# A graph layer on one Trainium2 core: the second group's transposes behind the first selection, the read-back on the other queue, ranks read by two engines, and a one-hot one use later

## The chip, the cores and the metric

One core of one Trainium2 chip runs the whole kernel. The metric is the device time of one execution in microseconds (us), the median of several runs.

## The reference

For 8 graphs of N = 1024 nodes with C = 128 features, and an adjacency matrix of 0 and 1:

```python
h = jnp.maximum(_layernorm(x, axis=-1), 0.0)
# per node: the first S = 25 neighbours by index
scores = jnp.where(A != 0, -jnp.arange(N), neg_inf)
vals, idx = jax.lax.top_k(scores, S)
feats = jnp.where((vals > neg_inf)[..., None], h[idx], neg_inf)
agg = feats.max(axis=2)
agg = jnp.where((degree <= S)[..., None], jnp.maximum(agg, 0.0), agg)
out = jax.nn.relu(jnp.concatenate([h, agg], axis=-1) @ W + b)
x + out
```

## The kernel before

The 8192 nodes are worked on in 16 groups of 512 rows, two groups to a graph (a batch). A group's way is this. The 0/1 adjacency is made a bf16 `mask`, and turned so that the neighbour index lies on the partitions (`mask_t`, 8 blocks of 128). **Selection**: `place(g, k)` on TensorE writes running counts of block k into the PSUM bank `side`, and `choose(g, k)` on ScalarE turns them into `chosen`, 1 where a neighbour is among the first 25. Block k + 1 needs `chosen` of block k, so this is a chain of TensorE and ScalarE. **Read-back**: `chosen` is stored to the DRAM tensor `kept` block by block and read back as `picks`, in which the neighbours of a partition are of another class (index modulo 8 instead of block). **Ranks**: `ranks` multiplies `picks` by `half_w` into one of two PSUM banks `ring`, and ScalarE (`stage`) reads it into `rank`, the running number of a neighbour in its class partition. **Picks**: for rank t = 1 to 4 and four pairs of classes, VectorE makes one-hots (`make_hot`, all 8 classes at once), `pick_pair` multiplies h (a high and a low f16 part) with them into `picked`, two buffers in turn, and `take_pair` on VectorE takes the maximum into `best`. The 16 pairs are called uses 0 to 15; the first two are copied by ScalarE (`first_maxima`). **Late ones**: neighbours of rank above 4 are marked in `late`, skewed over the partitions by seven DMAs of SP (`skew_late` into `late_skew`), ranked again (`late_ranks`), and picked in a loop whose length is read from data (`late_round` on TensorE; `take_late` and `make_late_hot` on VectorE). The first late one-hots are made ahead of that loop behind the uses in `LATE_HOT_USES`. At the end `project` multiplies by W, and `finish_group` adds x.

The order on each engine is written out by hand, and engines wait for each other by counting semaphores only. In the loop over groups, `step` interleaves: in uses 4 to 15 of group g lie ranks of group g + 1 (uses 6 to 13) and the selection of group g + 2 (uses 7 to 14). POOL makes h of the next batch in the odd groups but the last (`normalize`: lines 385, 388 and 391, then `fold_count`, then `low_part`, line 373, which writes `h_lo`); VectorE makes the high part behind use 10.

Ahead of the loop stands a prologue, in which groups 0 and 1 have no earlier work to hide behind. Their masks are turned by TensorE (`turn_blocks(g, q)`, 8 transposes for each quarter q) and copied out of PSUM. What the steps of the prediction touch, in the order of each engine:

- TensorE (lines 692 to 713): the transposes of group 0; `place(0, k)`, with `turn_blocks(1, 0)` to `(1, 2)` behind places 5, 6 and 7 and `(1, 3)` after them; two places of group 1; the 8 ranks of group 0, each of which waits for both halves of the read-back (`first_loaded`, line 602); then pairs 0 to 3 with places 2 to 5 of group 1 among them, places 6 and 7, and four late ranks.
- ScalarE (lines 502 to 524): two copies; `choose(0, k)` and the store of block k on ScalarE's own DMA queue; the square root of the variances (`spreads`) behind block 2; the read-back of the first 64 partitions (`first_picks(0)`, waits for the stores of blocks 0 to 3) behind block 6 and of the others (`first_picks(1)`, waits for blocks 4 to 7) behind block 7; two selections of group 1; the 8 rank reads; the rest of group 1's selection.
- VectorE (lines 864 to 908): the masks of group 0, two copies, statistics of x, the gain, W and the bias in parts, the masks of group 1 (line 781), h's high and low part, four copies for group 1 (line 897), the masks of group 2, then `make_hot(1, 0)`, which waits for all 8 rank reads, `make_hot(2, 0)`, and the late classes (lines 903 and 905).
- SP (lines 304 to 327): the loads; from line 315 it waits for the read-back, loads x of batch 1, turns the masks of group 2 by DMA, skews the late classes, stores group 1's `second_chosen` (it lies in `late_hot`) block by block, and reads it back (line 302).

## Time and profile before

| | us |
|---|---|
| median of 3 runs | 674.34 (673.2 to 675.48) |
| the profiled execution | 675.0 |
| its span, first to last instruction | 673.3 |
| busy in it: TensorE | 595.0 |
| VectorE | 601.3 |
| ScalarE | 403.3 |
| POOL (GpSimd) | 95.1 |

The profile is one execution. Busy times are unions over an engine's instructions; DMA-issuing, semaphore and register instructions are not counted as busy. PE is TensorE's matmul part and PEld its weight load, DVE is VectorE, ACT ScalarE, SP the queue that issues most DMAs. A row of the timeline has the start, the duration, the engine, the line, the operation, the tiles as out<-in, a count when neighbouring instructions are merged, and in brackets how long the engine had stood idle before it and what released it. The mean granted clock of TensorE over the span is 0.982 of full speed.

### The profile page before, as it was taken

What the parts mean: (1) busy time and instruction counts of PE and PEld (TensorE: products, weight loads), DVE (VectorE), ACT (ScalarE), POOL (GpSimd) and SP (SyncE); (2) the same over time, 40 slices, a digit from 0 to 9 for tenths busy, and PEclk for the clock granted to TensorE, in tenths of its full rate; (3) what the DMA queues carried; (4) which work ended last, traced back from release to release, by engine and by line L of the source; (5) the groups of instructions that cost most, each with busy time, mean ns of one, the idle gap of its engine ahead of it and who ended that gap; (6) DMA issues with size and microseconds to landing.
All of it is one profiled execution on the core that took longest, in us unless ns stands there. A gap on an engine that the chain in (4) does not pass through costs nothing.

```text
span 673.3 us, 9821 instructions
## 1 busy us (share of the span) xinstructions
PE 595.0 (88%) x2800; PEld 248.5 (37%) x2800; DVE 601.3 (89%) x727; ACT 403.3 (60%) x556; POOL 95.1 (14%) x142
## 2 busy tenths in 40 slices
PE   4457989899998999899998999899998999899986
PEld 2212334344433434343343434344443434343333
DVE  4844978999999999999999999999999999999996
ACT  3245855768277664857667685858667674836310
POOL 1300003200060000500051001500050000600000
PEclk9959999999999999999999999999999999999998
DMA  8456785658458383576657484566657352240100
GB/s 341 162 129 218 281 237 186 208 108 299 92 204 238 133 254 91 201 212 227 187 195 218 136 273 125 207 181 232 179 200 227 103 184 60 74 163 21 63 16 17
DMA packets 99438, 115.81 MB, mean 172 GB/s; under 512 B 66003, under 2 KB 85718, under 8 KB 94934
## 3 DMA queue, kind: packets, MB, share of 16 engines
q1 hardware_dynamic: 98102, 113.41, 53.1%
q10 hardware_dynamic: 1312, 2.10, 1.1%
q8 instruction: 12, 0.20, 0.1%
q14 instruction: 12, 0.10, 0.0%
HBM read 58.85 MB, written 20.97 MB: 119 GB/s over the span
## 4 chain that ended last, share of the span: by engine, by line
issue 40%; PE 25%; DVE 19%; POOL 8%; DMA 3%; ACT 3%; DVEq 1%; SPq 0%; POOLq 0%; ACTq 0%
DVE best L826 9%; PE picked L640 8%; PE picked L641 7%; PE ring L567 4%; DVE best L832 4%; POOL h L391 3%; DVE late_hot L838 2%; POOL h L385 2%; POOL h L388 2%; DVE hot L813 2%; PE final L667 1%; DMA picks<-kept 1%; PE final L671 1%; DMA adj_in<-in_adj_dram 1%; ACT late_rank L458 1%
## 5 line engine op out<-in xcount | busy, mean ns | idle before, releaser
L826 DVE TENSOR_TENSOR best<-picked,best 128x1024 f32<-128x1024 f32 x224 | 268.7, 1217 | 21.2 <-PE picked L641 20.2
L640 PE MATMUL picked<-hot,h_hi 128*128 128x512 f16 x512 | 196.3, 383 | 23.9 <-DVE best L826 14.7
L641 PE MATMUL picked<-hot,h_lo 128*128 128x512 f16 x512 | 196.0, 383 | 0.0
L640 PE MATMUL picked<-late_hot,hi_skew 128*128 128x512 f16 x344 | 130.5, 379 | 13.8 <-DVE late_hot L838 9.8
L641 PE MATMUL picked<-late_hot,lo_skew 128*128 128x512 f16 x344 | 130.3, 379 | 0.0
L458 ACT ACTIVATE rank<-ring,late_bias 128x512 bf16<-128x512 f32 x128 | 87.6, 688 | 52.6 <-PE ring L567 52.4
L832 DVE TENSOR_TENSOR best<-picked,best 128x1024 f32<-128x1024 f32 x86 | 105.1, 1222 | 15.4 <-PE picked L641 14.9
L458 ACT ACTIVATE late_rank<-ring,late_bias 128x512 bf16<-128x512 f32 x128 | 81.4, 687 | 57.4 <-PE ring L567 57.3
L466 ACT ACTIVATE chosen<-side,bias_cut 128x512 bf16<-128x512 f32 x120 | 81.9, 682 | 21.5 <-PE side L596 21.5
L640 PEld LDWEIGHTS picked<-hot,h_hi 128*128 128x128 f16 x512 | 50.3, 98 | 102.4 <-DVE best L826 32.9
L495 ACT COPY best<-picked 128x1024 f32<-128x1024 f32 x32 | 32.4, 1014 | 92.3 <-PE picked L641 92.3
L813 DVE TENSOR_SCALAR hot<-rank 128x4096 f16<-128x4096 bf16 x64 | 77.8, 1217 | 9.5 <-ACT rank L458 9.5
L838 DVE TENSOR_SCALAR late_hot<-late_rank,numbers 128x2048 f16<-128x2048 bf16 x86 | 75.2, 875 | 0.0
L641 PEld LDWEIGHTS picked<-hot,h_lo 128*128 128x128 f16 x512 | 50.4, 99 | 50.5 <-issue 1.6
L477 ACT ACTIVATE late<-rank,bias_late 128x1024 bf16<-128x1024 bf16 x60 | 63.8, 1136 | 0.0
L640 PEld LDWEIGHTS picked<-late_hot,hi_skew 128*128 128x128 f16 x344 | 33.4, 97 | 75.6 <-DVE late_hot L838 23.4
L411 POOL TENSOR_SCALAR late_other<-late_most 1x1 f32<-1x1 f32 x64 | 16.0, 251 | 285.7 <-DVE late_most L818 280.6
L567 PE MATMUL ring<-picks,half_w 128*128 128x512 bf16 x128 | 50.3, 395 | 5.3 <-DMA picks<-kept 4.3
L385 POOL TENSOR_TENSOR h<-x_in,moments 128x1024 f32<-128x1024 f32 x8 | 15.2, 1902 | 262.9 <-DVE gain L809 262.9
L453 ACT ACTIVATE mask<-adj_in 128x1024 bf16<-128x1024 uint32 x52 | 50.6, 1051 | 0.0
L596 PE MATMUL side<-mask_t,select_w 128*128 128x512 bf16 x120 | 47.5, 396 | 0.5 <-ACT mask_t L504 0.5
L595 PE MATMUL side<-mask_t,rest_w 128*128 128x512 bf16 x105 | 42.0, 400 | 5.9 <-ACT chosen L466 4.6
(85 smaller groups left out, 474.1 us busy)
## 6 DMA issues: line engine op xcount, KB each, us to landing
adj_in<-in_adj_dram SPq DMA_DIRECT2D x15, 2048.0 KB, 8.9
picks<-kept SPq DMA_DIRECT2D x15, 1024.0 KB, 5.0
kept<-chosen SPq DMA_DIRECT2D x112, 128.0 KB, 2.8
late_skew<-late SPq DMA_DIRECT2D x32, 192.0 KB, 3.4
x_in<-in_x_dram SPq DMA_DIRECT2D x8, 512.0 KB, 6.3
late_skew<-late SPq DMA_DIRECT2D x16, 256.0 KB, 4.6
late_skew<-late SPq DMA_DIRECT2D x32, 128.0 KB, 3.5
xres<-in_x_dram SPq DMA_DIRECT2D x16, 256.0 KB, 2.7
```

What stands on the lines that cost most here:

```text
L453: nc.scalar.activation(mask[:, q, :], counts, ACT.Sign).then_inc(mask_made, 1)
L458: nc.scalar.activation(dst[:, k, :], ring[k % 2][:, :], ACT.Relu, bias=bias).then_inc(ring_read, 1)
L466: nc.scalar.activation((second_chosen if second else chosen)[:, k, :], side[:, :], ACT.Sign, bias=bias_cut[:, 0:1], scale=-1.0).then_inc(c ...
L477: nc.scalar.activation(late[:, 2 * p:2 * p + 2, :], rank[:, s, 2 * p:2 * p + 2, :], ACT.Sign, bias=bias_late[:, 0:1]).then_inc(late_made, 1)
L567: last = nc.tensor.matmul(ring[k % 2][:, :], w[:, :], m, start=(i == 0), stop=(i == len(terms) - 1))
L596: nc.tensor.matmul(side[:, :], select_w[:, :], turned[:, k, :], start=(k == 0), stop=True, skip_group_check=True).then_inc(place_written, 1)
L640: nc.tensor.matmul(dst, hi[:, slot, k, :], onehot, start=start, stop=False)
L641: return nc.tensor.matmul(dst, lo[:, slot, k, :], onehot, start=False, stop=stop)
L813: nc.vector.tensor_scalar(hot[:, (t - 1) % 3, :, :], rank[:, s, :, :], float(t), None, ALU.is_equal).then_inc(hot_made, 1)
L826: nc.vector.tensor_tensor(best[:, half, s, :, :], picked[s][:, :, :], best[:, half, s, :, :], ALU.max).then_inc(picked_read, 1)
L832: nc.vector.tensor_tensor(best[:, s, i, :, :], picked[i][:, :, :], best[:, s, i, :, :], ALU.max).then_inc(late_read[i], 1)
L838: nc.vector.tensor_scalar(late_hot[:, part, :], late_rank[:, part, :], which, None, ALU.is_equal).then_inc(late_hot_made[i], 1)
```

## The change

The constant `LATE_HOT_USES` goes from (12, 14) to (13, 14): the first half of the late one-hots is made behind `take_pair` of use 13 instead of 12, in every group. The rest changes the prologue alone. TensorE does all transposes of group 1 behind the whole selection of group 0, then three places of group 1 instead of two, and waits for the read-back in front of its ranks. The ranks of group 0 are read by two engines, the even classes by ScalarE, which counts two at a time, and the odd ones by VectorE with an addition and a maximum on a semaphore of its own, `first_ranked`. ScalarE takes the square root behind block 1 instead of 2, and no longer issues the read-back; SP does, in two halves as before, ahead of its wait for `normed_made`, and waits for the landing only ahead of `store_chosen`. VectorE makes the masks of group 1 right behind the gain, ahead of the parts of W and of the bias.

```diff
--- before.py
+++ after.py
@@ -54,7 +54,7 @@
         return [[k for k in range(K) if use == first + k * (last - first + 1) // K] for use in range(USES)]
 
     SELECT_WITH, RANK_WITH = spread_over(7, 14), spread_over(6, 13)
-    LATE_EARLY, LATE_WITH, COUNT_WITH, COUNT_USE, LATE_HOT_USES = 4, {4: (4, 5), 5: (6, 7)}, (6, 7), 8, (12, 14)
+    LATE_EARLY, LATE_WITH, COUNT_WITH, COUNT_USE, LATE_HOT_USES = 4, {4: (4, 5), 5: (6, 7)}, (6, 7), 8, (13, 14)
     LATE_USES, HIGH_USE, TURN_USE = {14: (0, 1), 15: (2, 3)}, 10, 15
     STATS_USES, MOMENTS_USE, GAIN_USE = (9, 10), 12, 5
 
@@ -179,6 +179,7 @@
         first_stored = [sem(f"first_stored{i}") for i in range(2)]
         first_loaded = sem("first_loaded")
         ring_read = sem("ring_read")
+        first_ranked = sem("first_ranked")
         late_clamped = sem("late_clamped")
         late_made = sem("late_made")
         late_skewed = sem("late_skewed")
@@ -292,6 +293,12 @@
                     sp.wait_ge(chosen_made, chosen_due)
                     sp.dma_start(kept_by_block[k], (second_chosen if first else chosen)[:, k, :]).then_inc(chosen_stored, 16)
 
+            def first_picks(i):
+
+                part = slice(i * (P // 2), (i + 1) * (P // 2))
+                sp.wait_ge(first_stored[i], 16 * HALF)
+                sp.dma_start(picks[part, :, :], kept_by_class[part]).then_inc(first_loaded, 16)
+
             def load_picks(ranked):
 
                 sp.reg_add(stored_due, stored_due, LANDED)
@@ -312,13 +319,15 @@
             load_adj(1, 1)
             sp.wait_ge(mask_made, Q)
             load_adj(2, 0)
-            sp.wait_ge(first_loaded, 32)
+            for i in range(2):
+                first_picks(i)
             sp.wait_ge(normed_made, 1)
             load_x(1)
             for q in range(Q):
                 sp.wait_ge(mask_made, 2 * Q + q + 1)
                 sp.dma_start_transpose(mask_t[:, :, q * P:(q + 1) * P], mask[:, q, :]).then_inc(mask_turned, 16)
             skew_late(0)
+            sp.wait_ge(first_loaded, 32)
             store_chosen(True)
             load_picks(K)
             load_xres(0, 0)
@@ -465,12 +474,6 @@
                 act.wait_ge(place_written, g * K + k + 1)
                 nc.scalar.activation((second_chosen if second else chosen)[:, k, :], side[:, :], ACT.Sign, bias=bias_cut[:, 0:1], scale=-1.0).then_inc(chosen_made, 1)
 
-            def first_picks(i):
-
-                part = slice(i * (P // 2), (i + 1) * (P // 2))
-                act.wait_ge(first_stored[i], 16 * HALF)
-                act.dma_start(picks[part, :, :], kept_by_class[part]).then_inc(first_loaded, 16)
-
             def find_late(p, s, ranked):
 
                 act.wait_ge(ring_read, ranked)
@@ -504,21 +507,19 @@
                 nc.scalar.copy(mask_t[:, 2 * n:2 * n + 2, :], turned_bank[n]).then_inc(block_copied[0], 1)
             for k in range(K):
                 choose(0, k)
-                if k == 2:
+                if k == 1:
                     spreads(0)
                 act.wait_ge(chosen_made, k + 1)
                 act.dma_start(kept_by_block[k], chosen[:, k, :]).then_inc(first_stored[k // HALF], 16)
-                if k == K - 2:
-                    first_picks(0)
-            first_picks(1)
-            for k in range(2):
+            for k in range(3):
                 choose(1, k)
-            for k in range(K):
-                stage(0, k, rank[:, 0], late_bias[:, 0:1])
+            for k in range(0, K, 2):
+                act.wait_ge(ring_written, k + 1)
+                nc.scalar.activation(rank[:, 0, k, :], ring[0][:, :], ACT.Relu, bias=late_bias[:, 0:1]).then_inc(ring_read, 2)
             for s in range(2):
                 first_maxima(0, s, 0)
-                choose(1, 2 + s)
-            for k in range(4, K):
+                choose(1, 3 + s)
+            for k in range(5, K):
                 choose(1, k)
             for k in range(LATE_EARLY):
                 stage(K, k, late_rank, late_bias[:, k:k + 1])
@@ -598,9 +599,7 @@
 
             def ranks(g, at, k):
 
-                if isinstance(g, int) and g == 0:
-                    pe.wait_ge(first_loaded, 32)
-                elif k == 0:
+                if k == 0:
                     pe.wait_ge(picks_loaded, 16 * g)
                 accumulate(at, k, [(half_w, picks[:, k, :])])
 
@@ -695,20 +694,22 @@
                 turn_blocks(0, q)
             for k in range(K):
                 place(0, k)
-                if k >= K - 3:
-                    turn_blocks(1, k - (K - 3))
-            turn_blocks(1, Q - 1)
+            for q in range(Q):
+                turn_blocks(1, q)
             pe.wait_ge(chosen_made, K)
-            for k in range(2):
+            for k in range(3):
                 place(1, k)
+            pe.wait_ge(first_loaded, 32)
             for k in range(K):
-                ranks(0, 0, k)
+                if k > 1:
+                    pe.wait_ge(*((first_ranked, k // 2) if k % 2 else (ring_read, k)))
+                nc.tensor.matmul(ring[k % 2][:, :], half_w[:, :], picks[:, k, :], start=True, stop=True).then_inc(ring_written, 1)
             pe.wait_ge(lo_made, 1)
             for use in range(PAIRS):
                 pick_pair(0, use, 0)
-                place(1, 2 + use)
-            for k in range(2 + PAIRS, K):
-                place(1, k)
+                place(1, 3 + use)
+            place(1, K - 1)
+            pe.wait_ge(first_ranked, HALF)
             for k in range(LATE_EARLY):
                 late_ranks(0, K, k)
 
@@ -869,6 +870,8 @@
             stats_of(0, range(K))
             moments_of(0)
             make_gain(0)
+            for q in range(Q):
+                next_mask(1, q)
             dve.wait_ge(weights_loaded, 64)
             nc.vector.tensor_scalar(w_scaled[:, :, :], w_in[:, :, :], 1.0 / SCALE, None, ALU.mult).then_inc(consts_made, 1)
 
@@ -888,8 +891,6 @@
             dve.wait_ge(bias_step, 8)
             for q in range(Q):
                 nc.vector.tensor_copy(bias_parts[:, q * C:(q + 1) * C], bias_sum[:, 2, :]).then_inc(consts_made, 1)
-            for q in range(Q):
-                next_mask(1, q)
             high_part(0, 0)
             first_low()
             for n in range(PAIRS):
@@ -897,6 +898,10 @@
                 nc.vector.tensor_copy(rank[:, 1, 2 * n:2 * n + 2, :], turned_bank[n]).then_inc(second_copied, 1)
             for q in range(Q):
                 next_mask(2, q)
+            for k in range(1, K, 2):
+                dve.wait_ge(ring_written, k + 1)
+                nc.vector.tensor_scalar(rank[:, 0, k, :], ring[1][:, :], late_bias[:, 0:1], 0.0, ALU.add, ALU.max).then_inc(first_ranked, 1)
+            dve.wait_ge(first_ranked, HALF)
             dve.wait_ge(ring_read, K)
             make_hot(1, 0)
             make_hot(2, 0)
```

## Rows read from the trace of the kernel before

**Rows 1.** The page: busy time by engine; costliest groups; durations of one line (min/median/max).

```profile
PE 595.0 (88%) x2800; PEld 248.5 (37%) x2800; DVE 601.3 (89%) x727; ACT 403.3 (60%) x556; POOL 95.1 (14%) x142
...
L826 DVE TENSOR_TENSOR best<-picked,best 128x1024 f32<-128x1024 f32 x224 | 268.7, 1217 | 21.2 <-PE picked L641 20.2
...
L838 DVE TENSOR_SCALAR late_hot<-late_rank,numbers 128x2048 f16<-128x2048 bf16 x86 | 75.2, 875 | 0.0
...
L838 DVE TENSOR_SCALAR late_hot<-late_rank,numbers x86: 737/744/2362, 77.8 to 662.6; 128x2048 f16<-128x2048 bf16 x86
```

**Rows 2.** The chain of waits, its first 50 us: start, duration, what.

```profile
31.23 3.61 DMA kept<-chosen
34.86 4.64 DMA picks<-kept
...
45.86 1.24 DVE hot L813
```

**Rows 3.** The timeline of the prologue, 19 to 32 us.

```profile
19.00 1.90 POOL L385 TENSOR_TENSOR h<-x_in,moments 128x1024 f32<-128x1024 f32 x1 [16.45 <-DVE gain L809]
...
22.05 0.69 ACT L466 ACTIVATE chosen<-side,bias_cut 128x512 bf16<-128x512 f32 x1 [1.13 <-PE side L596]
...
26.04 2.48 DVE L781 TENSOR_SCALAR mask<-adj_in 128x1024 bf16<-128x1024 int32 x4
...
28.70 0.69 ACT L466 ACTIVATE chosen<-side,bias_cut 128x512 bf16<-128x512 f32 x1 [5.96 <-PE side L596]
...
30.27 1.47 PE L577 MATMUL picked<-eye,mask 128*128 128x128 bf16 x16
```

**Rows 4.** The timeline of an odd group, 110 to 125 us, VectorE and POOL.

```profile
110.72 3.58 DVE L826 TENSOR_TENSOR best<-picked,best 128x1024 f32<-128x1024 f32 x3
...
110.87 1.90 POOL L385 TENSOR_TENSOR h<-x_in,moments 128x1024 f32<-128x1024 f32 x1 [36.91 <-DVE gain L809]
...
120.29 2.12 POOL L373 TENSOR_TENSOR h_lo<-h,h_hi 128x1024 f16<-128x1024 f32 x1
...
120.60 2.36 DVE L838 TENSOR_SCALAR late_hot<-late_rank,numbers 128x2048 f16<-128x2048 bf16 x1
...
122.88 2.34 DVE L826 TENSOR_TENSOR best<-picked,best 128x1024 f32<-128x1024 f32 x2
```

**Rows 5.** DMA issues, us to landing: blocks 6, 7 and 3 of the first selection.

```profile
kept<-chosen ACTq DMA_DIRECT2D x1, 128.0 KB, 1.7
...
kept<-chosen ACTq DMA_DIRECT2D x1, 128.0 KB, 3.6
...
kept<-chosen ACTq DMA_DIRECT2D x1, 128.0 KB, 3.2
```

**Rows 6.** The first ranks: timeline; groups; a window (busy, PEclk, DMA share, GB/s).

```profile
39.55 1.03 PE L567 MATMUL ring<-picks,half_w 128*128 128x512 bf16 x2 [2.41 <-DMA picks<-kept]
...
40.20 1.27 ACT L458 ACTIVATE rank<-ring,late_bias 128x512 bf16<-128x512 f32 x2 [2.33 <-PE ring L567]
...
41.65 1.27 ACT L458 ACTIVATE rank<-ring,late_bias 128x512 bf16<-128x512 f32 x2 [0.19 <-PE ring L567]
...
L845 DVE SCALAR_TENSOR_TENSOR xres<-final,xres 128x512 f32<-128x512 f32 x16 | 11.1, 692 | 5.9 <-PE final L671 5.9
...
39.00:46.00 7.00, 4.52 (x8) 0.76 (x8) 0.14 (x1) 5.07 (x8) 0.00 (x0) 0.50 0.86 189
```

**Rows 7.** The timeline of group 0, use 6: the first rank of group 1.

```profile
66.92 0.39 PE L567 MATMUL ring<-picks,half_w 128*128 128x512 bf16 x1 [1.87 <-DMA picks<-kept]
```

**Rows 8.** The late skews of an odd group: timeline, and the last one's us to landing.

```profile
131.51 0.59 SPq L256 DMA_DIRECT2D late_skew<-late  x1
...
late_skew<-late SPq DMA_DIRECT2D x1, 192.0 KB, 3.7
...
135.92 0.59 PE L567 MATMUL ring<-late_skew,half_w 128*128 128x512 bf16 x2
...
137.78 0.10 PEld L567 LDWEIGHTS ring<-late_skew,half_w 128*128 128x128 bf16 x1 [0.68 <-ACT late_rank L458]
```

## The prediction

> **What bounds the kernel now.** I read the busy shares first: VectorE and TensorE are busy 89% and 88% of the span [rows 1], so the steady part is two nearly full engines that hand `picked` tiles to each other, and an idle microsecond inside it is rare. The unfilled time is at the front, so I read the chain of waits for its first 50 us: a store of 3.61 us, its read-back of 4.64 us, and the first VectorE one-hot only at 45.86 [rows 2]. The timeline of that stretch says why the store is late: ScalarE's selection of group 0 ran at a pitch of 0.69 + 1.13 = 1.82 us up to 22.05, then waited 5.96 us [rows 3]. TensorE had been put on `turn_blocks(1, 0)`, which waits for a mask that VectorE makes at 26.04, because the parts of the bias come first. Then I looked in the steady part for instructions much longer than their fellows: `late_hot` has 86, median 744 ns, longest 2362 ns [rows 1]. The mean of 875 ns gives (875 - 744) x 86 / (2362 - 744) = 7 long ones, one in each odd group that makes a new batch's h. There POOL's `h_lo` runs from 120.29 to 122.41, and the late_hot that starts at 120.60 ends at 122.96 [rows 4].
>
> **The front, step by step.** (a) With the transposes of group 1 behind `place(0, 7)`, blocks 6 and 7 follow at the pitch of 1.82: starts at 22.05 + 1.82 = 23.87 and 25.69, end 26.38. Before, block 7 was stored from 31.23 [rows 2]: 4.8 us earlier. The sqrt and its table load only move from behind block 2 to behind block 1, so one selection pays for it either way (nothing).
> (b) The read-back's halves move to SP. Before, the first half was issued on ScalarE's own queue between the stores of blocks 6 and 7; block 6 landed in 1.7 us, block 7 in 3.6 us [rows 5]. Block 3 is issued near 19.1 and lands 3.2 us later [rows 5], so SP can ask for the first half near 22.3, and it is nearly done when block 7 goes out at 26.4. I take 1.7 us, a landing at 28.1; the upper end is 3.6 (30.0). The second half, then 4.64 us as before [rows 2], lands at 32.8, at worst 34.7. Behind SP's wait stand x(1) and the mask transposes; they were behind the same landing before, so nobody loses. x(1) now shares the engines with the half: up to 0.5 us, by the distance between 1.7 and 3.6.
> (c) ScalarE no longer stands in a wait for stores, so `choose(1, 0..2)` run meanwhile. TensorE is free of group 0 at 25.7. The 32 transposes cost 1.47 us for 16 [rows 3] at the faster pace, up to 1.4 times that at the slower: 28.6 to 29.8. One copy (taken as one of the four masks that last 2.48 us together [rows 3]) and three place/choose rounds, two at 1.45 to 1.82, bring the third place to 33.0 to 34.2. It now stands ahead of the ranks in TensorE's order, so ranks start when the later of it and the read-back is there: I take 33.7, against 39.55 [rows 6].
> (d) VectorE makes the four masks from about 17.1, beside POOL's normalisation, which starts some 1.9 us earlier than 19.00 [rows 3], since the sqrt is one block earlier. The late_hot of 2362 ns [rows 4] shows that one of the two engines can wait out the other. Even all in series (2.5 us of masks, 6.9 us of POOL) the masks are there before 25.7 and h is ready by 27; the cover is some 2 us. If it is gone, each us counts in full.
> (e) Ranks split over two engines: less than it looks. A bank's round is read (0.69), signal, matmul: from ScalarE's 40.20 to 41.65 it is 1.45 us [rows 6], with only 0.19 us of idle, and two readers don't shorten a bank's round. What goes is ScalarE's turn on the second bank. VectorE reads 128x512 of PSUM in 692 ns [rows 6]. The last rank is ready 0.65 + 0.4 + 3 x 1.45 + 0.69 = 6.1 us after the start, against 45.86 - 39.55 = 6.3. The granted clock was 0.50 there (the 1.2 GHz level) [rows 6], after TensorE had stood idle for most of its wait for the read-back. Now it comes from transposes and places; at 2.4 GHz a round is some 0.2 us shorter, 5.0 us in all. I take 5.8.
> First one-hot: 33.7 + 5.8 = 39.5, which is **6.4 us earlier**; bounds 33.0 + 5.0 = 38.0 (7.9 us) and 34.9 + 6.2 = 41.1 (4.7 us).
> (f) Who carries it on: behind the one-hots SP issues seven skews and eight stores without a gap, then reads group 1's picks back, and TensorE waits 1.87 us for them at 66.92 [rows 7]. All of this hangs on the one-hots and on SP, so it moves with them. The last place of group 1 leaves the end of that chain (one fewer to do), but SP is later there: nothing more.
>
> **The late one-hots, steady part.** In an odd group with a new batch, take 12 ends at 120.65; `late_hot(0)` sits out POOL's `h_lo`. After the change take 13 goes there. It reads PSUM and one tile of SBUF, and three of its kind while POOL wrote `h` from 110.87 to 112.78 took 3.58 us, against 2.34 for two elsewhere [rows 4]. So take 13 runs 120.7 to 121.9, `late_hot(0)` waits for the same end and finishes at the same 122.96, and one take, a pair's 2.34 less one's mean of 1.21 to 1.22 = **1.13 us**, is gone from the path [rows 1, 4].
> What is late next: `late_skew`, whose making depends on ScalarE and SP, not on take 13, and stays where it is. The last of seven is issued at 131.51 and lands 3.7 us later, at 135.2; TensorE used it at 135.92 [rows 8]. So TensorE can come only some 0.6 us earlier there, not 1.13. But the second pair of these matmuls stood 0.68 us for ScalarE at 137.78, by its weight load [rows 8], and ScalarE's reads move by the full 1.13, so most of the lag is taken up: I take 1.03 us a group. Bounds: 0.5 (the lag goes through) and 1.13. Seven groups: **7.2 us**, from 3.5 to 7.9. In the other nine groups `late_hot(0)` and take 13 only change places while VectorE runs without a gap: nothing, within 0.1 each.
>
> A rule to weigh: the Trainium skill (SBUF — State Buffer, "SBUF: two separate sides") has it that VectorE in a two-port mode or with two SBUF inputs and GpSimd take one port pair for a whole instruction, and the other "fully blocks". The trace agrees for late_hot (2362 ns beside 744). By it a take, with one SBUF input, is free of this; if its SBUF input did count, rival B would hold.
> A rule that speaks against (b): the Trainium skill (DMA: Bandwidth & Descriptors, "Rules for kernel authors") says that spreading transfers over issuing engines doesn't help bandwidth, as they share the 16 engines. By it block 7 would gain only what the earlier start of the first half gives; this case's 1.7 and 3.6 us cannot tell the two apart.
>
> **Sum.** The profiled execution took 675.0 us, its span 673.3; the median of the runs is 674.34. 675.0 - 6.4 - 7.2 = 661.4, which is 660.7 on the median's scale. The known ends are 674.34 - 7.9 - 7.9 = 658.5 and 674.34 - 4.7 - 3.5 = 666.1.
>
> **Rivals.**
> A: the skews hold the steady part, each odd group gives 0.5. For: 135.2 against 135.92. Against: the idle time at 137.78. It gives 674.34 - 6.4 - 3.5 = 664.4.
> B: POOL's `h_lo` stops take 13 too (or late_hot meets the same delay elsewhere), so the one-hots give nothing: 674.34 - 6.4 = 667.9. Against: the takes from 110.72.
> C: the front gives little, since VectorE's early masks and POOL block each other, or the ranks wait for place(1, 2), or the second half lands late. With 3 us of the 6.4: 674.34 - 3 - 7.2 = 664.1; with nothing: 667.1.
> D, slower: TensorE's clock. It was at 0.50 from 39 to 46 [rows 6] (the 1.2 GHz level), after a stretch in which the engine mostly waited. Group 0's first matmuls now lie among places and ranks in another rhythm. If the level stayed low into group 0's uses, each matmul costs 1.03 - 0.61 = 0.42 us of pitch instead of 0.59 - 0.38 = 0.21 [rows 6, 8]; the 13.6 us are used up after 65 more matmuls at the low level. A whole group 0 (48 for its twelve uses and some 40 for its late rounds) would make 674.34 - 13.6 + 18.5 = 679.2. Against: the same dense picks follow behind the one-hots as before, and over the whole span TensorE's clock hardly shows below full.
> E: the change does not do what it says, because the order on TensorE leaves the wait at a mask (masks later than 25.7 + 4.8): 667, as C's end.
>
> **Chances.** Forecast 0.62; A 0.14; B 0.08; C and E 0.12; D 0.04. The range that holds 8 in 10 takes the sum's known ends, and half of B and C: 658.0 to 667.0. Below 0.3% (2 us) this kernel's measurement can't tell a change from none; the cases give faster 0.95, within 0.3% 0.02, slower 0.03.
>
> **What would show it.** ScalarE's blocks 6 and 7 at 23.9 and 25.7 with no wait of 5 us; the store of block 7 under 2.5 us; ranks from 33 to 34.5; the first one-hot at 39.5; TensorE's wait for picks in group 0 as long as before, all 6.4 us earlier. In odd groups a take beside `h_lo` of 1.22 us, then a late_hot of about 1.1 us, and a period of two groups 1.0 us shorter; TensorE waiting for `late_skew` there shows the lag. I am wrong on the front if masks of group 1 come after 25.7 or the second half lands after 35, and on the steady part if the longest take grows past 1.3 us or VectorE stands idle before the takes of the next group by what it saved.

## The result, and the profile after

The changed kernel takes 662.66 us (median of 5 runs, 660.67 to 664.44), the kernel before 674.34 us (672.96 to 675.48) beside it: a ratio of 0.9827, 95% interval 0.9804 to 0.9850. The forecast was 660.7 us in a range of 658.0 to 667.0. The profiled execution of the new kernel took 664.44 us with a span of 661.5, against 675.0 and 673.3.

The page of the kernel after (busy time by engine; then the take and the late one-hot, busy us and mean ns of one):

```profile
PE 596.5 (90%) x2800; PEld 249.8 (38%) x2800; DVE 597.0 (90%) x731; ACT 401.7 (61%) x552; POOL 96.3 (15%) x142
...
L827 DVE TENSOR_TENSOR best<-picked,best 128x1024 f32<-128x1024 f32 x224 | 270.0, 1218 | 23.3 <-PE picked L640 21.9
...
L839 DVE TENSOR_SCALAR late_hot<-late_rank,numbers 128x2048 f16<-128x2048 bf16 x86 | 66.5, 773 | 0.0
```

Against [rows 1], TensorE's busy time is 1.5 us longer, and VectorE's is 4.3 us shorter: the late one-hots lost 8.7 us (75.2 to 66.5), but four rank reads and the lengthened masks came in. Two parts can be told apart by where each group's result is added on VectorE (the read of `final` into `xres`, start in us):

| group | 0 | 1 | 3 | 5 | 7 | 9 | 11 | 13 | 14 | 15 |
|---|---|---|---|---|---|---|---|---|---|---|
| before | 105.7 | 141.8 | 220.8 | 299.8 | 374.8 | 449.9 | 525.0 | 603.9 | 640.9 | 670.1 |
| after | 99.7 | 134.7 | 213.0 | 291.0 | 365.5 | 439.6 | 513.5 | 591.5 | 628.5 | 658.3 |
| lead | 6.0 | 7.1 | 7.8 | 8.8 | 9.3 | 10.3 | 11.5 | 12.5 | 12.5 | 11.8 |

At the end of group 0 the lead is 6.0, each odd group adds 0.5 to 1.1, the even groups between them add nothing (up to 0.1 is lost), and the last one takes 0.7 back. This is one execution of each kernel. How far the end of group 0 scatters is told below: `e1_hot_only`, which has none of the front's edits, ends group 0 at 102.8.

The timeline of the prologue of after (start, duration, engine, line, operation, idle time before it and its releaser) answers [rows 3] and [rows 6]:

```profile
16.75 6.74 DVE L782 TENSOR_SCALAR mask<-adj_in 128x1024 bf16<-128x1024 int32 x4
16.91 2.28 POOL L394 TENSOR_TENSOR h<-x_in,moments 128x1024 f32<-128x1024 f32 x1 [14.36 <-DVE gain L810]
...
22.34 6.17 SPq L300 DMA_DIRECT2D picks<-kept  x2
...
23.67 0.69 ACT L475 ACTIVATE chosen<-side,bias_cut 128x512 bf16<-128x512 f32 x1 [1.19 <-PE side L597]
...
25.24 3.25 PE L578 MATMUL picked<-eye,mask 128*128 128x128 bf16 x32
...
25.48 0.69 ACT L475 ACTIVATE chosen<-side,bias_cut 128x512 bf16<-128x512 f32 x1 [1.12 <-PE side L597]
...
32.94 1.06 PE L706 MATMUL ring<-picks,half_w 128*128 128x512 bf16 x2
...
33.77 0.68 ACT L518 ACTIVATE rank<-ring,late_bias 128x512 bf16<-128x512 f32 x1
34.04 0.75 DVE L903 TENSOR_SCALAR rank<-ring,late_bias 128x512 bf16<-128x512 f32 x1 [0.48 <-PE ring L706]
...
35.22 0.69 ACT L518 ACTIVATE rank<-ring,late_bias 128x512 bf16<-128x512 f32 x1 [0.76 <-PE ring L706]
...
39.27 2.36 DVE L814 TENSOR_SCALAR hot<-rank 128x4096 f16<-128x4096 bf16 x2
```

The 5.96 us in which ScalarE waited for block 6 are gone, and the first one-hot stands at 39.27 instead of 45.86 [rows 2]. The store of block 7, issued at 26.20, lands in 1.8 us, where [rows 5] has 3.6. The DMA issues of that stretch are the first half of the read-back (issued at 22.34), then the stores of block 5 (22.50), block 6 (24.39) and block 7:

```profile
picks<-kept SPq DMA_DIRECT2D x1, 512.0 KB, 5.1
...
kept<-chosen ACTq DMA_DIRECT2D x1, 128.0 KB, 4.9
...
kept<-chosen ACTq DMA_DIRECT2D x1, 128.0 KB, 3.4
...
kept<-chosen ACTq DMA_DIRECT2D x1, 128.0 KB, 1.8
```

So the half lands at 27.4, and the three stores at 27.4, 27.8 and 28.0.

VectorE in an odd group of after, answering [rows 4]; POOL's `h_lo` runs from 114.28 to 116.40:

```profile
112.32 3.61 DVE L827 TENSOR_TENSOR best<-picked,best 128x1024 f32<-128x1024 f32 x3
115.84 1.11 DVE L839 TENSOR_SCALAR late_hot<-late_rank,numbers 128x2048 f16<-128x2048 bf16 x1
116.88 1.21 DVE L827 TENSOR_TENSOR best<-picked,best 128x1024 f32<-128x1024 f32 x1
```

The takes that run beside `h_lo` keep their length (three in 3.61, against 3.58 in [rows 4]); the late one-hot that meets its end is 1.11 us instead of 2.36.

### The profile page after: what moved, and what is told of

Its sections match the earlier page's. It is cut to its first block, busy times and chain, and to the rows that moved or that the text cites. A ratio compares the mean times of both kernels' runs of the same rounds, so it can differ in the third digit from the quotient of the medians.

```text
span 661.5 us, 9819 instructions
## 1 busy us (share of the span) xinstructions
PE 596.5 (90%) x2800; PEld 249.8 (38%) x2800; DVE 597.0 (90%) x731; ACT 401.7 (61%) x552; POOL 96.3 (15%) x142
## 3 DMA queue, kind: packets, MB, share of 16 engines
q10 hardware_dynamic: 1152, 1.05, 0.5%
## 4 chain that ended last, share of the span: by engine, by line
PE 53%; DVE 23%; issue 10%; DMA 5%; ACT 5%; SPq 2%; DVEq 1%; ACTq 0%
PE picked L639 17%; PE picked L640 15%; PE ring L568 9%; DVE best L827 8%; DVE late_hot L839 5%; DVE best L833 4%; PE final L666 2%; PE side L597 2%; PE side L596 2%; PE final L670 2%; DMA late_skew<-late 2%; DVE hot L814 2%; PE final L620 1%; DMA kept<-chosen 1%; ACT late L480 1%
## 5 line engine op out<-in xcount | busy, mean ns | idle before, releaser
L467 ACT ACTIVATE rank<-ring,late_bias 128x512 bf16<-128x512 f32 x120 | 82.5, 688 | 49.0 <-PE ring L568 48.8
L498 ACT COPY best<-picked 128x1024 f32<-128x1024 f32 x32 | 32.4, 1013 | 85.3 <-PE picked L640 85.3
L839 DVE TENSOR_SCALAR late_hot<-late_rank,numbers 128x2048 f16<-128x2048 bf16 x86 | 66.5, 773 | 0.0
L420 POOL TENSOR_SCALAR late_other<-late_most 1x1 f32<-1x1 f32 x64 | 16.1, 252 | 273.3 <-DVE late_most L819 268.2
L568 PE MATMUL ring<-late_skew,half_w 128*128 128x512 bf16 x128 | 42.1, 389 | 7.4 <-DMA late_skew<-late 4.4
```

What stands on the lines that cost most here:

```text
L467: nc.scalar.activation(dst[:, k, :], ring[k % 2][:, :], ACT.Relu, bias=bias).then_inc(ring_read, 1)
L568: last = nc.tensor.matmul(ring[k % 2][:, :], w[:, :], m, start=(i == 0), stop=(i == len(terms) - 1))
L839: nc.vector.tensor_scalar(late_hot[:, part, :], late_rank[:, part, :], which, None, ALU.is_equal).then_inc(late_hot_made[i], 1)
```

## The experiments

**Each part alone.** `e1_hot_only` is the kernel before with the two late one-hots at uses 13 and 14. `e2_front_only` is the kernel after with them back at 12 and 14.

```diff
-    ... LATE_HOT_USES = 4, {4: (4, 5), 5: (6, 7)}, (6, 7), 8, (12, 14)
+    ... LATE_HOT_USES = 4, {4: (4, 5), 5: (6, 7)}, (6, 7), 8, (13, 14)
```

> The kernel before with the one edit in the steady part: the first late one-hots behind use 13 instead of 12. My theory (one take of 1.13 us goes under POOL's h_lo, less a lag at the late skews in some groups): 6 to 7 us faster than before, the longest late_hot 1.1 us instead of 2.36, no take longer than 1.25. Rival (POOL stops the take too, or the next wait gives it all back): within 2 us of before.

> The changed kernel with the late one-hots back behind uses 12 and 14, so the prologue's edits alone. Theory: the prologue gives 6.4 us at the first one-hot and hands on 5.5 to 6.0, so 5.5 to 6 us faster than before; and this run and the one with the other part alone add up to the whole 11.7. Rival (the two parts share a gain or stand in each other's way at the late skews): the sum of both is off by 2 us or more.

Measured: 667.02 us for the one-hots alone (ratio 0.9905, 0.9871 to 0.9939) and 669.7 us for the front alone (0.9931, 0.9910 to 0.9952). Here is the first late one-hot of an odd group on VectorE in `e1_hot_only`, then in `e2_front_only`:

```profile
115.36 3.61 DVE L826 TENSOR_TENSOR best<-picked,best 128x1024 f32<-128x1024 f32 x3
118.89 1.11 DVE L838 TENSOR_SCALAR late_hot<-late_rank,numbers 128x2048 f16<-128x2048 bf16 x1
```

```profile
114.04 2.38 DVE L839 TENSOR_SCALAR late_hot<-late_rank,numbers 128x2048 f16<-128x2048 bf16 x1
```

The late one-hot is 1.11 us where the uses are 13 and 14 and 2.38 where they are 12 and 14, whatever the front. The odd groups take 35.0 us in the one and 36.1 in the other, and the first one-hot stands at 45.79 and 39.57. The gains of the parts, 7.5 and 4.8 us against the runs of before beside them (674.49), add up to 12.3, and the whole gives 11.7: no sign that they share a gain, within the 1 to 2 us by which single executions of this kernel differ. The split between them is less sure. The one-hots gave a little more than the 6 to 7 us expected, the front less than its 5.5 to 6, although the one profiled execution of `e2_front_only` ends group 0 6.6 us ahead of before (99.2 against 105.7).

**Is the wait POOL's `h_lo`?** `e8_double_hlo` lets POOL make `h_lo` twice, the first time into a spare tile, so that the second write lies across `late_hot(0)`.

```diff
+ nc.gpsimd.tensor_tensor(spare[:, slot, :, :], h32[:, :, :], h_hi[:, slot, :, :], ALU.subtract).then_inc(spared, 1)
  nc.gpsimd.tensor_tensor(h_lo[:, slot, :, :], h32[:, :, :], h_hi[:, slot, :, :], ALU.subtract).then_inc(lo_made, 1)
```

> The changed kernel with POOL's h_lo done twice in each odd group, once into a spare tile (the result is the same). Theory (the two engines wait for each other on late_hot but not on a take): the take beside it stays at 1.21 to 1.23 us, the late_hot behind it grows from 1.11 to about 3.2 us, 2 us in each of seven groups, and the whole is 10 to 14 us slower than the changed kernel. Rival (late_hot was long for another reason, such as TensorE or a DMA): late_hot stays at 1.11 and the whole within 2 us. Second rival (takes are stopped too): a take of 2 us or more shows.

Measured: 678.76 us (1.0050, 1.0031 to 1.0068), 16.1 us over the kernel after, more than the 10 to 14 expected. POOL first, then VectorE in an odd group:

```profile
113.58 2.12 POOL L384 TENSOR_TENSOR spare<-h,h_hi 128x1024 f16<-128x1024 f32 x1
115.67 2.12 POOL L385 TENSOR_TENSOR h_lo<-h,h_hi 128x1024 f16<-128x1024 f32 x1
```

```profile
111.62 3.61 DVE L830 TENSOR_TENSOR best<-picked,best 128x1024 f32<-128x1024 f32 x3
115.14 3.19 DVE L842 TENSOR_SCALAR late_hot<-late_rank,numbers 128x2048 f16<-128x2048 bf16 x1
```

The takes run through POOL's first piece untouched. The late one-hot that starts at 115.14 ends at 118.33, when the second piece is done (117.79) plus about half a microsecond of its own. It is 2.08 us longer than in the kernel after, for 2.12 us of POOL more. Seven of these are 14.6 of the 16.1 us. That is not all that happens: the seven odd groups take 17.4 us more together. In four of them, 3.0 to 3.1 us longer each, TensorE's mean granted clock is 0.96, and 1.00 in the other three, which are 1.5 to 2.1 us longer, and in all seven of the kernel after. (In the first of the four it is 0.77 from 118 to 122 us, behind an idle time of TensorE of 2.71 us; it stood as long in the second odd group, without such a fall.) So about 4 us, by an estimate from these lengths, are the slower clock. Rival B, by which a take beside `h_lo` waits too, is excluded.

**What in the front gives the time?** `e12_order_only` is the kernel before with one edit on TensorE.

```diff
                 place(0, k)
-                if k >= K - 3:
-                    turn_blocks(1, k - (K - 3))
-            turn_blocks(1, Q - 1)
+            for q in range(Q):
+                turn_blocks(1, q)
```

> The kernel before with one edit: TensorE turns the whole of group 1's masks after place(0, 7). The late one-hots, the read-back queue, the place and the split of the rank reads stay as they were. My theory (half of the front's gain is the order, the other half the store of block 7 and the read-back): blocks 6 and 7 are read from the bank at about 23.9 and 25.7 us, block 7's store still waits on ScalarE's queue behind the first half of the read-back and lands at about 30, the ranks start at about 34.5, the first one-hot at about 41 (4.8 us earlier than 45.86), and the whole is 4 to 5 us faster than before: about 670. Rival, the order is the whole of it: first one-hot at 39.3 to 39.8 and the whole at about 669. Rival, the masks of group 1, which end at about 26 us on VectorE, hold the transposes and what stands behind them: first one-hot no earlier than 43, the whole within 3 us of before.

Measured: 669.21 us (0.9911, 0.9877 to 0.9945). Its timeline:

```profile
25.71 0.69 ACT L466 ACTIVATE chosen<-side,bias_cut 128x512 bf16<-128x512 f32 x1 [1.13 <-PE side L596]
26.00 2.48 DVE L780 TENSOR_SCALAR mask<-adj_in 128x1024 bf16<-128x1024 int32 x4
...
35.32 1.04 PE L567 MATMUL ring<-picks,half_w 128*128 128x512 bf16 x2 [1.83 <-DMA picks<-kept]
...
41.63 2.36 DVE L812 TENSOR_SCALAR hot<-rank 128x4096 f16<-128x4096 bf16 x2 [6.49 <-ACT rank L458]
```

At the first one-hot, order alone gives 45.86 - 41.63 = 4.2 of the 6.6 us, where 4.8 were expected. Block 7 is read at 25.71, no later than with the whole change (25.48), although the masks still come at 26.00. The other 2.4 us are the store and read-back: block 7's store took 4.1 us here and 1.8 there. They can't be found again in the whole. The median is 5.9 us below before's (675.14 beside it), and `e2_front_only`, with the whole front, is 4.8 below (674.49), with intervals that overlap; group 0 ends at 99.9 here and at 99.7 in the kernel after. So no run shows what the rest of the front adds to the order in the whole. `e4_act_readback`, next, shows only what one part of it costs when it is undone in another order of transfers.

`e4_act_readback` is the kernel after with the two halves of the read-back on ScalarE's queue again, the first behind block 6's store and the second behind block 7's.

```diff
-            for i in range(2):
-                first_picks(i)                                  # SyncE
...
+                if k == K - 2:
+                    first_picks(0)                              # ScalarE, in the loop of stores
+            first_picks(1)
```

> The changed kernel with the read-back's halves issued by ScalarE again, on its own queue. Theory: ScalarE then waits for the stores and group 1's three selections come behind that, so the ranks wait for the third place of group 1 and not for the read-back: stores land at 30 instead of 28, read-back at 34.5, the three places behind ScalarE's wait till about 34; the first one-hot 2 to 3 us later than 39.27 and the whole 2 to 3 us slower. Rival (the queue makes no difference, all came from the order of the transposes): within 0.5 us of the changed kernel.

Measured: 666.34 us (0.9876, 0.9845 to 0.9908), 3.7 us over the kernel after, and the first one-hot at 44.66, so 5.4 us late; 2 to 3 were expected for both. The chain of waits of `e4_act_readback`, with SyncE's and ScalarE's issues ahead of it, shows why:

```profile
24.92 0.33 SPq L249 DMA_DIRECT2D x_in<-in_x_dram  x1
24.93 0.50 ACTq L473 DMA_DIRECT2D picks<-kept  x1
```

```profile
26.38 6.22 DMA kept<-chosen
32.62 5.78 DMA picks<-kept
...
44.66 2.36 DVE hot L815 x2
```

With the read-back gone from SyncE, nothing held SyncE's load of x(1) back, and it went out at 24.92 beside the first half, just ahead of block 7's store. The half, which took 5.1 us in the kernel after and 4.7 in `e12_order_only`, took 7.5 here, and the store that went out behind it 6.2, against 4.1 in `e12_order_only`. In all four kernels block 7's store lands 0.1 to 0.8 us behind the first half: at 34.8 and 34.7 in before, 30.5 and 29.7 in `e12_order_only`, 32.6 and 32.4 here, 28.0 and 27.4 in the kernel after. There the half has its own queue, and block 5's store, which follows it by 0.16 us, still takes 4.9 us. So what the move to SyncE gives the store is that the half goes out 2.6 us earlier (22.34 against 24.98), ahead of the stores of blocks 5 and 6, and that its wait holds x(1) back. The two causes of the 5.4 us (the later half, x(1)) were not run apart.

**Parts that I costed near nothing.** `e3_one_reader` gives all eight rank reads to ScalarE again, `e5_masks_late` puts group 1's masks back behind the bias parts, and `e6_two_places` leaves two places of group 1 ahead of the ranks instead of three.

```diff
-            for k in range(0, K, 2):        # e3, ScalarE (VectorE's odd ones go too)
+            for k in range(K):
...
-            for q in range(Q):              # e5, VectorE: from behind the gain ...
-                next_mask(1, q)
...
+            for q in range(Q):              # ... to ahead of high_part(0, 0)
+                next_mask(1, q)
...
-            for k in range(3):              # e6, TensorE and ScalarE alike
+            for k in range(2):
```

> The changed kernel with all 8 first ranks read by ScalarE again. Theory (two readers don't shorten a bank's round of 1.45 us, they only take ScalarE's turn off the second bank): the first one-hot comes 0.2 to 0.5 us later than 39.27, the whole is at most 0.5 us slower. Rival (the split halves the reads and is worth much of the prologue's gain): the one-hot 2 us later or more.

> The changed kernel with group 1's masks made behind the parts of the bias again, as before the change. Theory (what cost 4.8 us was TensorE's order, which stood the transposes ahead of two places; the masks' own time only matters if they come after 25.2): POOL now starts 2 us earlier, so the bias parts end near 24 and the masks near 26.5; the transposes run into the last masks by 1 us or less, and the first one-hot comes 0 to 1 us later than 39.27. Rival (the early masks are the gain): 3 us later or more.

> The changed kernel with two places of group 1 ahead of the ranks instead of three. Theory (the read-back lands near 32.8 and the third place ends near 32.9, so both are equally late): the ranks start at most 0.3 us earlier than 32.94, the first one-hot likewise, and the whole is the same within 0.5 us. Rival (the third place held the ranks up): 1 us earlier.

Measured: 662.02 (0.9805, 0.9778 to 0.9832), 661.14 (0.9794, 0.9764 to 0.9824) and 661.22 us (0.9795, 0.9766 to 0.9825); none can be told from the kernel after. In `e3_one_reader` ScalarE reads all eight without a gap and the one-hot comes at the same time, not 0.2 to 0.5 us later as expected:

```profile
33.81 5.42 ACT L467 ACTIVATE rank<-ring,late_bias 128x512 bf16<-128x512 f32 x8
39.26 2.36 DVE L811 TENSOR_SCALAR hot<-rank 128x4096 f16<-128x4096 bf16 x2 [5.67 <-ACT rank L467]
```

In `e5_masks_late` POOL is undisturbed and the masks come after the selection, with the one-hot at 39.55:

```profile
19.19 1.90 POOL L397 TENSOR_TENSOR h<-h,gain 128x1024 f32<-128x1024 f32 x1
...
24.25 2.48 DVE L782 TENSOR_SCALAR mask<-adj_in 128x1024 bf16<-128x1024 int32 x4
```

In `e6_two_places` TensorE is free early and stands 1.57 us for the read-back, until 33.08; with three places it starts the ranks at 32.94. The third place fills a wait and is worth no time here.

**Do the late skews hold the odd groups?** TensorE waits for a late skew to land three times, 4.4 us in all, where it was once and 2.3 us in the kernel before. `e9_split_skew` issues the last chain's two transfers from ScalarE's queue. `e7_both_at_14` makes both late one-hots behind use 14.

```diff
-                    skew_late(g + 1)                            # e9, SyncE
+                    skew_late(g + 1, range(CHAINS - 1))
...
+                if more:                                        # e9, ScalarE: the last chain
+                    act.dma_start(late_skew[CHAINS - 1::CHAINS, ...], late[...]).then_inc(late_skewed, 16)
...
-    ... LATE_HOT_USES = ..., (13, 14)                           # e7
+    ... LATE_HOT_USES = ..., (14, 14)
```

> The changed kernel with the last two of the seven late skews of each group issued by ScalarE's queue in place of SP's, in the loop over groups. Theory (in some odd groups the lag that was left is the late skews' landing): TensorE no longer waits for late_skew in odd groups, they give up to 0.5 us more in one or two of seven, group 0's end comes about 1 us earlier, and the whole is 1 to 2 us faster than the changed kernel. Rival (the skews land by their share of the DMA engines and not by SP's issues): the waits stay and the whole is the same within 0.7 us.

> The kernel after with both late one-hots behind use 14. If the wait is for GpSimd's piece of h_lo and for that alone, the first late one-hot of an odd group then starts after that piece has ended and takes 0.74 us, not 1.11, so that VectorE is done with both some 0.3 us earlier; with TensorE free to use it, up to 0.4 us less in each of seven odd groups: 660 against 662.7. Rival, the late skews no longer leave room (TensorE already waits 3.0 to 4.4 us in the whole run for a late skew to land, and both now start later by a take): the odd groups keep their 35.0 us or grow, and the whole stays at 662.7 or goes to 664.

Measured: 660.53 us (0.9779, 0.9752 to 0.9805) for the split, whose waits stayed (4.9 us, five times): the issues are not what is late, the landing is. Its median is 2.1 us below the kernel after's, but `e5_masks_late` and `e6_two_places`, measured beside the same runs of before, are 1.5 us below it too, so this is no gain of the split that can be told. For both at 14, 659.64 us (0.9763, 0.9733 to 0.9794). VectorE in the odd group of `e7_both_at_14`:

```profile
112.01 3.61 DVE L827 TENSOR_TENSOR best<-picked,best 128x1024 f32<-128x1024 f32 x3
115.90 1.22 DVE L827 TENSOR_TENSOR best<-picked,best 128x1024 f32<-128x1024 f32 x1 [0.29 <-PE picked L640]
117.05 1.41 DVE L839 TENSOR_SCALAR late_hot<-late_rank,numbers 128x2048 f16<-128x2048 bf16 x2
```

The late one-hot no longer waits (0.74 instead of 1.11), but VectorE now catches up with TensorE and stands 0.29 us for the take. From the three takes to the first take of the late rounds it is 120.63 - 112.01 = 8.62 us, and 120.94 - 112.32 = 8.62 in the kernel after. The trace shows no gain, though the median lies 3.0 us below the kernel after's; its profiled execution was the slowest of its six (663.31). The interval lies below the change's all the same (0.9733 to 0.9794 against 0.9804 to 0.9850), so what the median gained is open.

**What holds the end of group 0?** Of the 6.6 us at the first one-hot, 6.0 arrive at the end of group 0, and that end moves by over 3 us between variants whose first one-hots agree within 0.3 us (96.4 in `e5_masks_late`, 99.7 here). The DMA issues of after from 64 to 96 us (KB each, us to landing) have the load of group 4's adjacency ahead of the stores, read-back and late skews of the next groups:

```profile
adj_in<-in_adj_dram SPq DMA_DIRECT2D x2, 2048.0 KB, 10.8
kept<-chosen SPq DMA_DIRECT2D x8, 128.0 KB, 11.3
...
late_skew<-late SPq DMA_DIRECT2D x1, 256.0 KB, 6.3
```

`e11_adj_later` moves the load of group g+4 behind the late skew of group g+1 in every step, `e15_first_adj_later` in the step of group 0 alone (on top of `e7_both_at_14`).

```diff
-                if not at_end(it, u, 4):                        # both; e15 for group 0 alone
-                    load_adj(g + 4, u % 2)
...
                     skew_late(g + 1)
+                if not at_end(it, u, 4):
+                    load_adj(g + 4, u % 2)
```

> The kernel after with the adjacency load of group g+4 asked for behind the late skew of group g+1 on the same queue, not ahead of it. Theory: the stretch from the last take of group 0 to its end, 10.0 to 12.5 us from one execution to the next, is set by stores and skews that share the 16 DMA engines with the adjacency load; then group 0 ends 1 to 3 us earlier than 99.7 us, and the whole is 1 to 3 us faster than after. Rival, the skews land no sooner, since the engines carry other transfers anyway: group 0 ends at 99 to 100 and the whole stays within 1 us of 662.7. Against it: the load of an adjacency block comes so late that its group waits for it, and the groups behind grow longer.

> The kernel after with both late one-hots behind use 14, and with group 4's adjacency load alone (the one asked for in the step of group 0) behind the late skew of group 1; every other adjacency load keeps its place. For this, SyncE's first round of four groups is written out ahead of its loop. With all the loads moved, group 0 ended at 95.3 instead of 99.7, but groups 2 and 4 took 45.1 and 46.5 us instead of 42.9 and 43.1, and the gain was gone by group 4. Theory: group 0 gains since its 12 late-skew and store transfers no longer share the engines with the load, and groups 2 and 4 lost through the loads of their own steps; then group 0 ends at 95 to 97, group 2 takes 43, and the whole is 655 to 657. Rival: the load of group 4 lands late for its masks, or the mask transposes of the second step run into it, and group 2 gives the 3 to 4 us back: the whole is 659 to 661, as with the late one-hots behind use 14 alone.

Measured: 665.74 us (0.9847, 0.9812 to 0.9882) with all of them moved. Group 0 ends at 95.3, 4.4 us earlier, but groups 2 and 4 take 45.1 and 46.5 us instead of 42.9 and 43.1, and TensorE waits for transposed masks (five times, 5.4 us), which it did not in the kernel after. With the first alone moved: 659.29 us (0.9768, 0.9743 to 0.9792). The same DMA issues there, and the end of group 0:

```profile
adj_in<-in_adj_dram SPq DMA_DIRECT2D x2, 2048.0 KB, 8.1
kept<-chosen SPq DMA_DIRECT2D x8, 128.0 KB, 6.2
...
late_skew<-late SPq DMA_DIRECT2D x1, 256.0 KB, 3.8
```

```profile
96.25 0.69 DVE L855 SCALAR_TENSOR_TENSOR xres<-final,xres 128x512 f32<-128x512 f32 x1 [0.22 <-PE final L679]
```

Group 0 ends 3.5 us earlier, groups 2 and 4 take 42.9 and 43.1 again, and the last group ends at 654.5 against 658.3. So the load did hold the stores and the skews: with it in its old place the stores take 11.2 us at the median in `e5_masks_late` too. What that is worth in the whole is not shown. The expectation was 655 to 657 us; the result is the time of the rival. The interval lies below the change's, as that of `e7_both_at_14` does, which this version contains, and the two can't be told apart (659.29 and 659.64). In the traces it is 3.2 us ahead of `e7_both_at_14` at the end of group 0 (96.2 against 99.4), but `e5_masks_late` ends at 96.4 with the load in its old place.

The clock is the other part of that scatter. Here is the first matmul that reads `late_skew` in that stretch of the kernel after, and the clock behind it (us, PE busy, ..., PEclk, DMA share, GB/s), then the same in `e5_masks_late`:

```profile
92.50 0.78 PE L568 MATMUL ring<-late_skew,half_w 128*128 128x512 bf16 x2 [2.98 <-DMA late_skew<-late]
...
92.00:98.00 6.00, 5.50 (x18) 2.27 (x19) 2.55 (x3) 2.65 (x4) 0.00 (x0) 0.72 0.78 155
```

```profile
91.06 0.38 PE L568 MATMUL ring<-late_skew,half_w 128*128 128x512 bf16 x1 [2.47 <-DMA late_skew<-late]
...
92.00:98.00 6.00, 6.00 (x36) 3.57 (x35) 4.95 (x5) 2.46 (x4) 0.00 (x0) 1.00 0.49 100
```

A mean of 0.72 over 6 us is about 3.4 us at 0.50, the 1.2 GHz level. From that matmul to the end of group 0 it is 7.2 us in before, in the kernel after and in `e7_both_at_14`, which have such a stretch, and 5.3 us in `e5_masks_late` and `e1_hot_only`, which don't. So 1.9 us of the scatter are the clock, and the rest is when the skew lands. TensorE had stood idle for it just before, 2.98 us in the kernel after and 2.26 in before, but also 2.47 and 2.41 in the two without the fall, so these traces don't tell which execution gets it. Of the 3.2 us of `e15_first_adj_later`, 1.8 are the earlier start of these matmuls (90.37, without a wait, against 92.19) and 1.3 the shorter stretch behind them, at a clock of 1.00.

## Why the prediction was right, step by step

| step | forecast | measured |
|---|---|---|
| (a) blocks 6, 7 read at | 23.87, 25.69 | 23.67, 25.48 |
| (b) block 7's store to landing | 1.7 | 1.8 |
| (c) ranks start | 33.7 | 32.94 |
| (e) start of ranks to one-hot | 5.8 | 6.3 |
| first one-hot earlier by | 6.4 | 6.6 |
| (f) handed on to group 0's end | all | 6.0 |
| odd groups, seven | 7.2 | 6.5 |
| last group | 0 | -0.7 |

(a) held, and its reason too: TensorE was held by its order alone (`e12_order_only`). (b) The forecast took the lower end for the store, and it came, for the reason given: the half had 1.2 us left when block 7 went out. What counts is when the half starts and what else is in flight, not which queue the store has to itself: 1.8, 4.1 and 6.2 us for the same 128 KB.

(c) and (e) were each off by half a microsecond or more, in opposite directions, so that the first one-hot comes within 0.2 us of the forecast is in part luck. The ranks start early because TensorE turned the masks at the fast pace (3.25 us for 32, done at 28.5 where 28.6 was the early end). They take as long as before, 6.3 us, since the pace of a bank is unchanged: ScalarE's reads start at 33.77 and 35.22, 1.45 us apart as in [rows 6]. I had counted on ScalarE's turn on the second bank to go away. Instead VectorE's read costs 0.75 us, not the 0.692 of the nearest row, and one reader for all banks is as fast (39.26). The granted clock stood at 0.50 from 34 to 38 us again (0.67 from 30 to 34), although TensorE had come from transposes and places; the guess that these would keep it at 2.4 GHz was wrong (us, PE busy, ..., PEclk, DMA share, GB/s):

```profile
34.00:38.00 4.00, 2.67 (x7) 0.62 (x6) 2.25 (x3) 1.83 (x3) 0.00 (x0) 0.50 1.02 193
```

(d) The masks and POOL do block each other, as the late one-hot's row led me to fear: four masks take 6.74 us instead of 2.48, and POOL's first piece 2.28 instead of 1.90. The last mask ended at 23.5 and the transposes began at 25.2, so the cover of some 2 us hid it, as costed, and `e5_masks_late` shows that the early masks buy nothing in return. Rival C (the front gives little) has fallen with that, and E (the order leaves the wait) with (a).

(f) The lead is 6.75 us at the first rank of group 1 (60.17 against 66.92), 6.2 at SyncE's next read-back (82.98 against 89.14) and 6.0 where TensorE gets the late skew (92.50 against 98.52), so the 0.6 us go in what SyncE issues and lands. TensorE's wait for that skew was 2.98 us, and 2.26 before. That 6.0 of 6.6 arrived is a reading of one execution of each, where this end moves by 3 us: `e1_hot_only` ends group 0 3.0 us ahead of before with the same first one-hot. The agreement with "all" is no closer than that.

The odd groups: from one to the next the lead grows by 1.12, 0.64, 0.98, 0.53, 1.05, 1.11 and 1.03 us, 6.5 in all. Five of them lie around the 1.03 us that I took. In these five the odd group alone gives 1.11, so the skews take nothing there, and the even group behind it loses up to 0.13. The two short ones are those in which TensorE stood for a late skew, here the first:

```profile
207.47 0.60 PE L568 MATMUL ring<-late_skew,half_w 128*128 128x512 bf16 x2 [0.65 <-DMA late_skew<-late]
```

So rival A was true in two groups of seven, near its 0.5 us. The term's mechanism was right and its size was over by 0.7 us, since I let the skews be as late in every group as in the one that I read. In `e9_split_skew` the waits stay with fewer issues on SyncE, so the landing is the limit.

The last 0.7 us are TensorE's clock in the last projection, which no step had. Eight matmuls took 2.08 us, against 1.42 before; the granted clock of that stretch was 0.50, and 0.77 before. It is not the change's doing: `e6_two_places` and `e7_both_at_14` have 1.16 us there, and `e12_order_only` 2.08.

```profile
656.22 2.08 PE L670 MATMUL final<-w_scaled,agg_t 128*128 128x128 f32 x8 [1.97 <-DVE agg_t L962]
...
656.00:658.40 2.40, 2.08 (x8) 1.78 (x8) 0.23 (x2) 0.00 (x0) 0.00 (x0) 0.50 0.00 0
```

Rival D, the clock as a brake on group 0, came in part, at a fraction of its 18.5 us. The 0.50 in the ranks and the fall ahead of the end of group 0 are in before too. But there is one more in the kernel after: 0.72 over 50 to 56 us (0.50 from 52 to 54), behind an idle time of 1.18 us, where before has 1.00 over 56 to 62. It cost nothing that shows, since TensorE waited 1.13 us for the read-back at 60.17 anyway. Two small slips in the prediction's working change nothing: the landing at 135.2 and the use at 135.92 are 0.7 us apart, not 0.6, and no row gives the 34.9 and 6.2 of the upper bound, where its own steps have 34.7 and 6.1.

On the two rules of the Trainium skill. By its page "SBUF — State Buffer" (two separate sides) only an operation of VectorE in a two-port mode or with two SBUF inputs takes the port pair that GpSimd uses. The takes, with one SBUF input, agree (3.61 us for three beside GpSimd). The late one-hots of 1.11, 2.38 and 3.19 us agree only if they run in a two-port mode, and no run here shows their mode. The rule of "DMA: Bandwidth & Descriptors", that spreading transfers over issuing engines gives no bandwidth, agrees with the skews (`e9_split_skew`: the waits stay) and with the stores: with the half on another queue, block 5's store lands with the half, after 4.9 us, and block 7's store gains by the half's earlier start.

## What to carry to other kernels

Where an engine waits in a prologue, look at what its order puts ahead of the work it has, before its speed: one moved loop gave two thirds of what the whole front gave at the first one-hot, and in the run time the two can't be told apart. Splitting reads over two engines gave nothing, because each bank's round stayed the same. A lead at the start of a stretch is not yet time saved: read it again where the stretch ends, in more than one execution. In a steady part, an instruction that is three times its usual length names the partner that it meets; put beside that partner an instruction that reads what it doesn't hold. And when a wait moves off a queue, ask what else it was holding back.

## What the runs showed of the hardware

A 128 KB store that went out while a 512 KB read-back half was in flight landed 0.0 to 0.8 us behind that half, on the half's queue or on another: it took 4.9, 3.4 or 1.8 us when it followed the half by 0.16, 2.05 or 3.86 us on the other queue, 3.6 and 4.1 us when it followed by 1.45 us on the same one, and 6.2 us when a 512 KB load was in flight as well. A 2 MB load issued ahead of eight 128 KB stores let them take 11.3 us each at the median, and 6.2 when it was issued behind the skews.

VectorE and POOL lengthen each other: four masks took 6.74 us instead of 2.48 beside three pieces of POOL, which took 2.28, 2.22 and 3.04 us instead of 1.90, 1.90 and 2.85 (`e5_masks_late`).

SyncE's issue of a late skew took 1.78 us once in the kernel after and 1.68 once before (and an issue of `hi_skew` there 1.78, at 218.39), where the median is 0.60; `e5_masks_late`, `e6_two_places` and five others have none of it among the first skews. With it the adjacency load goes out some 0.7 us later (65.62 against 64.77 and 64.93), and nothing in the trace says where it comes from.
